# VectorE's chains cut into single steps, and new call lists for all engines in a three-stage decoder layer

## What is computed

```python
x = _layernorm(x + _L0_attn_ref(x, ...))               # a state space block (input projections, 4 tap convolution,
                                                       # decays exp(cumsum), chunks, gate, RMS norm, output projection)
x = _layernorm(x + _L0_xattn_ref(ctx_1024, x, ...))    # attention: 8 heads, 256 queries on 120 context rows and the 256 tokens
x = _layernorm(x + _L0_ffn_ref(x, ...))                # below
```

```python
gf = _global_net(x.mean(axis=1, keepdims=True), ...)
out = x
for _ in range(3):
    tf = _coupling_net(out, ...)                       # gelu, gelu, gelu, sigmoid: 256 -> 256 -> 128 -> 64 -> 1
    coupling = 0.1 + adaptive_range * ((0.7 * gf + 0.3 * tf) - 0.5) * 2.0
    out = out + coupling * _twist(out)
```

## Time and profile before

| | us |
|---|---|
| median of 3 runs | 3863.9 (3862.89 to 3865.1) |
| span of the profiled execution | 3861.4 |
| around it, median less span | 2.5 |

### The profile page before, as it was taken

How to read it: one execution, slowest core, us unless ns; L and a number is a source line. 1 busy time by engine, 2 the same in 40 slices (tenths; PEclk the granted TensorE clock), 3 DMA queues, 4 the chain that set the end, 5 groups by cost and what they waited for, 6 DMA issues and landing times.

```text
span 3861.4 us, 77375 instructions
## 1 busy us (share of the span) xinstructions
PE 3783.3 (98%) x25728; PEld 3000.9 (78%) x25728; DVE 3286.2 (85%) x8098; ACT 3237.9 (84%) x7812; POOL 1748.5 (45%) x3084
## 2 busy tenths in 40 slices
PE   6999999999999999999999999999999999999997
PEld 5777877877877878778778778777787787787775
DVE  7888888888888888888888888888888888888874
ACT  5788888888888888888888888888888888888885
POOL 3444445354454444453544544534535445445442
PEclk8999999999999999999999999999999999999998
DMA  3111112111211111121111111111211211111110
GB/s 97 54 47 59 55 45 61 54 42 58 58 45 55 48 59 54 45 61 53 43 57 59 45 55 50 56 55 45 61 55 42 61 55 45 55 54 53 55 38 17
DMA packets 312350, 203.14 MB, mean 53 GB/s; under 512 B 55056, under 2 KB 310928, under 8 KB 311952
## 3 DMA queue, kind: packets, MB, share of 16 engines
q1 hardware_dynamic: 311952, 198.20, 17.5%
HBM read 180.17 MB, written 17.96 MB: 51 GB/s over the span
## 4 chain that ended last, share of the span: by engine, by line
PE 59%; ACT 16%; DVE 15%; issue 4%; POOL 4%; DMA 1%; SPq 0%; DVEq 0%; POOLq 0%
PE psum L253 20%; PE psum L428 8%; PE psum L338 6%; PE psum L463 5%; PE psum L438 5%; PE psum L452 4%; PE psum L325 4%; ACT prob L979 3%; ACT h L1021 2%; ACT L979 2%; ACT L1021 2%; PE psum L497 2%; ACT xc L891 2%; POOL rs_mix L2175 2%; DVE nmax L1638 1%
## 5 line engine op out<-in xcount | busy, mean ns | idle before, releaser
L979 ACT ACTIVATE prob<-psum,nmax 128x376 f32<-128x376 f32 x1024 | 585.2, 575 | 49.5 <-DVE nmax L1638 46.2
L1638 DVE TENSOR_REDUCE nmax<-psum 128x1 f32<-128x376 f32 x1024 | 541.5, 540 | 14.4 <-PE psum L428 11.0
L2139 POOL TENSOR_TENSOR Lm<-Lm,G 128x384 f32<-128x384 f32 x512 | 506.1, 1012 | 92.8 <-DVE out_sb L1741 68.4
L438 PE MATMUL psum<-ident,prob 128*128 128x128 f32 (+1 forms) x3072 | 480.5, 276 | 2.1 <-ACT probT L989 1.1
L1442 DVE SCALAR_TENSOR_TENSOR u<-psum,par,u 128x253 f32<-128x253 f32 (+5 forms) x960 | 449.1, 479 | 28.1 <-ACT u L882 1.7
L428 PE MATMUL psum<-kT,q_sb 64*128 64x376 f32 x2048 | 467.7, 528 | 0.2 <-ACT prob L979 0.2
L438 PEld LDWEIGHTS psum<-ident,prob 128*128 128x128 f32 (+1 forms) x3072 | 363.0, 141 | 73.9 <-issue 45.0
L989 ACT ACTIVATE probT<-psum 128x384 f32<-128x384 f32 x512 | 252.7, 494 | 182.7 <-PE psum L438 182.5
L2126 POOL TENSOR_SCALAR_AFFINE_SELECT Lm<-Lm 128x256 f32<-128x256 f32 x512 | 205.7, 435 | 411.6 <-DMA Lm<-cum_row 411.6
L253 PE MATMUL psum<-x_hi,w_in_hi 128*128 128x256 f32 (+1 forms) x1152 | 360.9, 313 | 22.5 <-DVE w_in_lo L1764 9.3
L452 PE MATMUL psum<-probT,V 128*64 128x256 f32 (+1 forms) x3072 | 375.0, 385 | 0.3 <-ACT probT L989 0.3
(11 more groups left out here) (222 smaller groups left out, 11157.9 us busy)
## 6 DMA issues: line engine op xcount, KB each, us to landing
Lm<-cum_row SPq DMA_DIRECT2D x64, 1024.0 KB, 5.2
Lm<-cum_row SPq DMA_DIRECT2D x64, 512.0 KB, 6.5
invT<-inv_row SPq DMA_DIRECT2D x256, 128.0 KB, 3.0
xT_sb<-in_xT SPq DMA_DIRECT2D x64, 256.0 KB, 3.1
x_sb<-in_x SPq DMA_DIRECT2D x64, 256.0 KB, 3.3
result<-out_sb SPq DMA_DIRECT2D x64, 256.0 KB, 2.2
inv_row<-inv_t SPq DMA_DIRECT2D x512, 1.0 KB
ctx_sb<-in_ctx SPq DMA_DIRECT2D x64, 120.0 KB, 2.7
```

Of the source, the lines that this page charges most:

```text
L438: t = tr(banks[b][0:m, j * P:(j + 1) * P], prob[:, r, j0:j0 + m], ident[:, :])
L979: act(prob[:, r, :], b[:, 0:NK], ACT.Exp, bias=nmax[:, n:n + 1], accum_out=psum_row[:, n:n + 1]).then_inc(a_exp, 1)
L1638: e.tensor_reduce(nmax[:, n:n + 1], banks[bank_of["sc", s, n]][:, 0:NK], AX.X, ALU.max, negate=True).then_inc(d_max, 1)
L2139: t = tt(Lm[:, h, :], Lm[:, h, :], G[:, :], ALU.mult)
```

## The change

Every waiting chain of DVE is cut at its waits into calls of one step each: `conv(s, c)` becomes `conv_tap(s, c, 0..2)`, `bcdt` becomes three `bcdt_tap` and `dt_add`, `bc` becomes `bc_silu`, `bc_high`, `bc_low`, `cum` becomes `cum_dt`, `cum_da`, `cum_scan`, and so on; `cycle` becomes `gain`, `twisted_part` and `pre`. The instructions, their tiles and their shapes stay. `d_u`, one semaphore for the taps of four channels, becomes four. `spread_cum` waits for `set_w` 3 too, since its target overlaps the raw weights. `x1_keep` now waits for `l_mix` itself, the bank of PE's `bcdt` is free only after the taps too, and `twisted_part` and `pre` wait for `a_hb` and `a_ha` in both cycles.

Then the call lists of all five engines are new: other orders within a pass, passes that are turned (the loop's body of DVE, POOL and SP now holds work of `f - 2`, `f - 1`, `f`, `a`, `m`), and another start and end. The number of calls of PE, ACT, POOL and SP is the same. The core of the diff:

```diff
-            def taps(src, c, rows, done, at):
-                for n, d in enumerate((1, 2, 3)):
-                    stt(u[0:rows, c, d:L], src[:, 0:L - d], prm("conv_w", 4 * c + 3 - d, slice(0, rows)),
-                        u[0:rows, c, d:L], ALU.mult, ALU.add).then_inc(done, 1)
-                    if n < 2:
-                        ve.wait_ge(done, at + n + 1)
+            def tap(src, c, rows, n, done, s):
+
+                d = n + 1
+                ve.wait_ge(done, 3 * s + n)
+                stt(u[0:rows, c, d:L], src[:, 0:L - d], prm("conv_w", 4 * c + 3 - d, slice(0, rows)),
+                    u[0:rows, c, d:L], ALU.mult, ALU.add).then_inc(done, 1)
...
                 sp.wait_ge(d_cum, s + 1)
+                sp.wait_ge(set_w, 3)
                 sp.wait_ge(cum_in, 32 * (s - 1))
```

More of the change, by code:

```diff
@@ L561, in _ @@
             y_pair(0, 1)
-            ctxT(0)
             y_pair(0, 2)
+            y_pair(0, 3)
+            bcdt(1)
             in_x(1, 0)
-            y_pair(0, 3)
-            in_x(1, 1)
             out_proj(0)
             mean_square(0)
+            in_x(1, 1)
             x1T(0)
+            q_pair(0, 0)
+            k_tile(0, 0)
+            k_tile(0, 1)
+            k_tile(0, 2)
+            xcT(1, 0)
+            xcT(1, 1)
+            scores(0, 0, 0)
+            ctxT(1)
+            v_tile(0, 0)
@@ L588, in _ @@
[L588 to L597, removed]
+            y_pair(1, 0)
+            y_pair(1, 1)
+            k_tile(0, 3)
+            turn(0, 2)
+            scores(0, 1, 1)
+            y_pair(1, 2)
+            y_pair(1, 3)
+            scores(0, 2, 0)
+            bcdt(2)
+            turn(0, 3)
@@ L598, in _ @@
+            in_x(2, 0)
+            scores(0, 2, 1)
+            turn(0, 4)
+            out_proj(1)
+            mean_square(1)
+            v_tile(0, 1)
+            turn(0, 5)
+            scores(0, 3, 0)
+            turn(0, 6)
             v_tile(0, 2)
[L599 to L602, removed]
             turn(0, 7)
             turn(0, 8)
+            x1T(1)
+            in_x(2, 1)
             values(0, 0)
-            y_pair(1, 2)
@@ L607, in _ @@
-            y_pair(1, 3)
+            values(0, 1)
+            scores(0, 3, 1)
             turn(0, 9)
-            bcdt(2)
+            q_pair(1, 0)
             turn(0, 10)
[L611 to L621, removed]
-            k_tile(1, 0)
-            xcT(2, 0)
@@ L634, in _ @@
                 q_pair(a, 1)
-                cb(m)
+                k_tile(a, 3)
+                turn(a, 2)
                 scores(a, 1, 0)
[L637 to L643, removed]
                 y_pair(m, 0)
                 y_pair(m, 1)
[L646 to L649, removed]
+                scores(a, 1, 1)
@@ L682, in _ @@
                 layer(f, 1, 1)
+                turn(a, 10)
                 k_tile(m, 0)
[L684 to L697, removed]
@@ L703, in _ @@
+            in_z(last, 0)
+            layer(last - 3, 2, 1)
+            turn(last - 2, 14)
+            ctxT(last)
+            turn(last - 2, 15)
+            layer(last - 3, 2, 2)
+            values(last - 2, 2)
+            values(last - 2, 3)
             scores(last - 1, 0, 1)
-            xcT(last, 1)
-            k_tile(last - 1, 3)
+            turn(last - 1, 0)
+            layer(last - 3, 2, 3)
             cb(last)
-            scores(last - 1, 1, 0)
+            v_tile(last - 1, 0)
@@ L771, in _ @@
+            layer(last - 2, 2, 2)
+            scores(last, 0, 1)
+            layer(last - 2, 2, 3)
+            v_tile(last, 0)
+            w_o(last - 1, 0)
+            scores(last, 1, 0)
+            turn(last, 0)
             w_o(last - 1, 1)
             q_pair(last, 1)
[L773 removed]
             turn(last, 1)
@@ new lines, in _ @@
+            context_n(last)
+            x_silu(last, 1)
+            by_token(last)
+            top(last - 2, 15)
+            x_dt(last, 0)
+            gain(last - 3, 1)
+            twisted_part(last - 3, 1)
+            pre(last - 3, 1)
+            inverse(last - 2, 1)
+            top(last - 1, 0)
+            turn_inverse(last - 2, 1)
+            out_norm(last - 4, 0)
+            turn_out(last - 2, 12)
+            x_dt(last, 1)
+            bc_silu(last)
+            top(last - 1, 1)
```

1718 lines of the change are left out of this document (1006 added, 712 removed).

## The result

The changed kernel takes 3801.82 us (median of 4 runs, 3800.57 to 3802.82), the kernel before 3863.81 beside it: a ratio of 0.9839 (95% interval 0.9825 to 0.9853), 62 us less. I had forecast 3826, 38 us less, within 3798 to 3882.

The account below looks back on a forecast made before the run. TensorE's list was taken to set the loop: 57.75 + 0.1 + 0.3 + 0.1 = 58.25 us a pass against 58.95, 43 us less in 61 passes, ends +5, so 3863.9 - 38 = 3826 us, range 3798 to 3882.

Parts of the forecast that it names:

- What bounds the kernel: TensorE's own list sets the loop; other lists pay only where PE waits, at the ends, or where PE's order gets cheaper.
- The clean pass before: PE's old order: 57.92 us a pass without any wait, so 58.95 holds 1.03 us of waits.
- The clean pass after: PE's 70 calls in the new order, 29 boundaries being new pairs: 57.75 us a pass, 0.17 less.
- The waits: PE's waits in the new pass: 0.1 left before layer(2,1), 0.3 at new places, 0.1 for what is left.
- The slow passes: Passes lengthened by a late load, 0.13 us a pass; should go, as SP issues load_xT and load_ctx earlier.
- The sum: A pass of 58.25 us against 58.95, 43 us less in 61 passes, ends +5: 3826 us.
- My own signs: Right: passes 58.1 to 58.4 us, 508 loads, ACT near 3319, out_norm near 410 ns; wrong: regular wait before v_tile(a,2).
- ACT's list: 63 more table loads, 508 in all, 81 us of ACT, covered by its idle time except before v_tile(a,2).
- Rival (b): Slower: ACT's chain Ln, load, exp, load is on the path; 3904 with a full load uncovered; chance 0.21.
- DVE's chains: Separating chained DVE operations saves some 0.1 us each, 0.5 to 1 us a pass, no time of PE.
- DVE beside POOL: out_norm apart from times_g falls from 732 ns towards 408, saving 0.65 us of DVE a pass, hidden.
- The ends: Start +3 us (weights(0,3) before conv(0,0)), end +2 (layers before w_o(63)): together +5, between -6 and +15.

Follow-up runs that it names:

- old_norm_apart2: old_loads_first with DVE's out_norm(f, 0) also moved to the end of the pass, away from POOL's times_g: 3862.61 us, ratio 0.9994 to the kernel before.
- turn5_first: The changed kernel with one swap on ACT, turn_out(a, 5) before layer(f, 0, 0): 3784.35 us, ratio 0.9794 to the kernel before.
- exp10_early: turn5_first with exp(a, 10) before softplus(m + 1) on ACT and top(f, 10) before x2_high(f - 1) on DVE: 3823.49 us, ratio 0.9896 to the kernel before.
- old_loads_first: The kernel before with SP's three loads for the next sequence ahead of store(f) instead of behind it: 3863.41 us, ratio 0.9994.

## Why the prediction was right, and where it wasn't

*What bounds the kernel.* Right: PE's list sets the pass, and time taken off another engine away from PE's waits pays nothing (`old_norm_apart2`). Taken off or added at such a wait, it counts: 17.5 us less in `turn5_first`, 39 more in `exp10_early`.

*The clean pass before.* Right: 57.92 by the smallest boundaries, 57.99 in the run of PE alone. The waits that I named add up to 0.98, which leaves 0.05 of my 1.03 for the passes with a late load, where I counted 0.13 for them further on; they cost 0.11.

*The clean pass after: the step that failed.* I had 57.75 and it is 57.01. Two of the pairs that I took to occur in the old order too, and so to have a price in the trace, don't occur inside its loop, and I priced them by a place behind the loop that has a wait in it. `values` to `scores` stands in the old timeline at 3767.67, and in the new one inside the loop at 1804.34:

```profile
3767.67 1.49 PE L428 MATMUL psum<-kT,q_sb 64*128 64x376 f32 x4
3769.09 0.54 PE L438 MATMUL psum<-ident,prob 128*120 128x128 f32 x3
```

```profile
1804.34 0.90 PE L429 MATMUL psum<-kT,q_sb 64*128 64x376 f32 x4
1805.17 0.54 PE L439 MATMUL psum<-ident,prob 128*120 128x128 f32 x3
```

The same four matmuls take 1.42 us up to the `turn` there and 0.83 here. I priced the pair at 0.73, and it is 0.32. The trace of before had that price too, in a second place ahead of the loop:

```profile
118.98 0.90 PE L428 MATMUL psum<-kT,q_sb 64*128 64x376 f32 x4
119.81 0.54 PE L438 MATMUL psum<-ident,prob 128*120 128x128 f32 x3
```

There the four take 0.83 us, and the boundary from `values` is 0.32. So for this pair I didn't take the smallest in the trace, as my rule said. `q_pair` to `layer(1,1)` stands in the old trace only once, behind the loop; I priced it at 0.61, and it is 0.34. Together that is 0.69 of the 0.74. Of the 29 new pairs the prediction prices three singly: `w_o` to `w_o` 0.43, `in_x` behind `bcdt` 0.23, `scores` to `bcdt` 0.63. They came out at 0.43, 0.23 and 0.59. So the order is worth 0.98 us a pass, where I had 0.17: the term was mis-sized by 0.8.

*The waits.* The forecast of 0.5 us was 0.88, so this term missed the other way. `k_tile(a,1)` and `layer(2,2)` wait no more, as said. `layer(2,1)` kept 0.25 us, not 0.1: ACT runs without a pause from the table load behind `layer(1,2)` to `h`, and DVE's steps weren't the late ones. `v_tile(a,2)` waits 0.32, which is the 0.3 that I took for new waits, at the place named. `layer(1,1)` (0.16) and `v_tile(a,0)` (0.12) I hadn't seen. `y_pair(2)` doesn't wait. On `v_tile(a,2)` I gave ACT's chain 8.9 to 9.2 us from `x2_turn` to the end of `turn_out(a,5)`, and a room up to 9.35; in the pass shown it ended 9.66 behind (1766.67 to 1776.33). The slow passes nearly went (0.11 to 0.03 us on the mean). `old_loads_first` bears out the reason that I gave, loads too close to their use, for the waits before `bcdt`; by itself it gained nothing, since other waits came. Rows 8 show the load of `xT`; the 0.6 us that I gave for a `spread_inv` stand in no row there.

*The sum.* 57.75 + 0.5 = 58.25 against 57.01 + 0.88 = 57.89. The two errors go against each other, and the larger one is the order's. So the time was right in sign and range, but by luck and not for my reason: the order, to which I gave 0.17 of a gain of 0.70 us, made 0.98 of 1.06, and the waits, to which I gave 0.53, made 0.08.

*My own signs.* The 508 loads and `out_norm` near 410 ns came as said. The pass (57.89, for 58.1 to 58.4), the wait before `layer(2,1)` (0.25, for at most 0.15) and ACT's busy time (3304.6, for 3319) did not, and the regular wait before `v_tile(a,2)`, which I had named as a sign of being wrong, is there.

*ACT's list.* 508 loads, as counted: 251 + 189 + 64 and four single ones. ACT is busy 66.7 us longer (81 forecast), and the time fell. The Trainium skill (ScalarE: Activation LUTs, section "Table sets: the hidden batching unit") would have the list batched by set; here the added load reaches PE only through `turn_out(a,5)`, and one swap on ACT, with all 508 loads kept, took that back (`turn5_first`). The prediction says that the trace's loads agree with the skill's price. They take 1283 ns each, and the next activation follows at once (the load at 1773.82, `h` at 1775.12); that section's own figure, about 2.7 us a load, isn't borne out here. Rival (b) had the right chain and the right place; a third of a microsecond of it was uncovered, not a full load.

*DVE's chains.* In the timeline of DVE two chained taps and a tap apart from its neighbour:

```profile
1769.87 0.99 DVE L1453 SCALAR_TENSOR_TENSOR u<-psum,par,u 128x255 f32<-128x255 f32 x2
...
1771.15 0.47 DVE L1453 SCALAR_TENSOR_TENSOR u<-psum,par,u 128x253 f32<-128x253 f32 x1
1771.55 0.53 DVE L1686 TENSOR_REDUCE nmax<-psum 128x1 f32<-128x376 f32 x1
```

0.40 us to the next operation where it isn't needed, 0.50 in the chain: the 0.1 that I took from rows 11. DVE's busy time fell by 38 us, just below the 40 to 90 forecast. Added up one by one its operations take 43 us more than before (3590.7 to 3633.5), so 81 us more of them overlap, 1.3 a pass where I had 0.5 to 1; longer operations took half of it back.

*DVE beside POOL.* `out_norm` fell from 732 ns to 411, 41 us in all, as said. But `ncum` (before: 166 ns, now 319), `x_lo` (742 to 1203) and `out_x` (367 to 519) rose by 39, 29 and 19 us, and POOL's busy time by 62. All three now run beside a POOL operation on `Lm` (`ncum` alone still takes 166 ns): the contention moved to other operations. No wait of PE in the table is known to lead back to one of them, but no run of the changed kernel takes them apart.

*The ends.* +5 forecast, 3 to 4 measured. The first `y_pair` comes 6.4 us later (45.27 for 38.83) and `x1T(0)` 0.1 earlier, for 5 and 1 later forecast.

## What to carry to other kernels

Where one engine is busy 98% of the span, run its list alone, without waits, in both orders before speaking of waits: here the two lists alone were 63 us apart, and the two kernels 62. A price read from the trace is only a price if it comes from many places with their smallest value in the loop; one occurrence at the end of the program can hold a wait. A call moved up in an in-order queue to serve a waiting engine must itself be ready there, and what stands behind it moves too, perhaps beside an operation of another engine that slows it: three of my own edits cost 22 to 188 us where they were meant to save or to change nothing. And an edit that leaves the time as it was may still have taken the wait away: `old_loads_first` did, and another wait took its place.

## What the runs showed of the hardware

The two matmuls of a pair that use different halves of the array start 7 ns apart (`scores` on 64 rows, `values` and `y_pair` on 64 columns); over the whole array they start 0.32 us apart (`scores`) and 0.22 (`values`). Taking `scores` over 128 rows with the same count of matmuls makes the pass 3.3 us longer, `values` over 128 columns 4.9.

A change between whole array, half of the rows and half of the columns mostly costs about 0.1 us at the first matmul behind it: `turn` to `scores` 0.20 on 64 rows and 0.11 on 128, `y_pair` to `scores` 0.20 and to `y_pair` 0.10, `values` to another call 0.31 and to `values` 0.21. Only `scores` to `y_pair` or `values` shows none, 0.41 as before any call. Behind a half-array call the second matmul of most whole-array calls comes 0.05 to 0.11 us later than behind a whole-array one (`turn` 0.16 for 0.11, `w_o` 0.32 for 0.22).

A DVE cast of 128x512 took 0.42 us where it started before a POOL operation and 1.22 where it started 0.33 us behind one.
